# A convolution and mixture-of-experts block on one core: the experts in two passes, weights laid out on the host, and another order in the last iteration

## What is computed

```python
x = x + conv_ref(ln_c(x), ...)          # layer norm over channels, group norm, w1, relu, w2, residual
t = to_tokens(x)                        # 8 batches, 16384 tokens of 64 numbers
t = t + ffn_ref(ln_t(t), ...)           # layer norm over the 64 numbers of a token
# ffn_ref, per batch: 32 experts, each takes its K = 8 best tokens
logits = einsum('bsd,ed->bse', x, gate_w) + gate_b
vals, idx = top_k(softmax(logits, axis=1).transpose(0, 2, 1), 8)
pooled = einsum('bked,bke->bed', gathered, topv)
h = gelu(einsum('ebd,edh->ebh', [pooled, 1], weight1))   # weight1: 32 x 65 x 256
out = einsum('ebh,eho->ebo', [h, 1], weight2)            # weight2: 32 x 257 x 64
outputs = zeros.at[flat_idx].add(out * topv)             # 256 rows per batch
```

## Time and profile before

| | |
|---|---|
| median of 3 executions | 684.8 us (681.87 to 685.7) |
| the profiled execution: its own time, its span | 687.47 us, 685.7 us |
| busy share: PE, DVE, ACT, POOL | 79%, 71%, 62%, 27% |
| mean granted clock of the tensor engine | 0.893 |
| chain that ended last | PE 41%, DVE 36%, issue 8%, ACT 7% |

### The profile page before, as it was taken

How to read it: one execution, slowest core, us unless ns; L and a number is a source line. 1 busy time by engine, 2 the same in 40 slices (tenths; PEclk the granted TensorE clock), 3 DMA queues, 4 the chain that set the end, 5 groups by cost and what they waited for, 6 DMA issues and landing times.

```text
span 685.7 us, 13882 instructions
## 1 busy us (share of the span) xinstructions
PE 542.0 (79%) x5630; PEld 274.8 (40%) x5630; DVE 488.5 (71%) x946; ACT 426.1 (62%) x597; POOL 185.4 (27%) x110
## 2 busy tenths in 40 slices
PE   3569988988988898889888898989888476623981
PEld 1234444443444344444444443444334132321781
DVE  5674566898789688978897889688976276785120
ACT  1455787779767876797779777877796353431100
POOL 1008080216022502250244024302433500011044
PEclk9857999999999899999999999899999979955555
DMA  8940445344624462447145713471125941100000
GB/s 196 200 100 32 123 125 162 115 125 123 173 75 124 124 173 74 125 123 184 64 124 150 189 59 108 138 190 57 40 92 132 200 94 62 63 4 5 1 13 18
DMA packets 35428, 73.38 MB, mean 107 GB/s; under 512 B 12292, under 2 KB 14372, under 8 KB 31268
## 3 DMA queue, kind: packets, MB, share of 16 engines
q1 hardware_dynamic: 34340, 71.44, 38.8%
q0 software_dynamic: 1024, 1.05, 0.6%
HBM read 38.40 MB, written 34.08 MB: 106 GB/s over the span
## 4 chain that ended last, share of the span: by engine, by line
PE 41%; DVE 36%; issue 8%; ACT 7%; DMA 2%; another core or an unknown queue 2%; POOL 1%; SPq 0%; DVEq 0%; ACTq 0%; POOLq 0%
PE st L364 10%; DVE xs L856 7%; PE cv L375 6%; PE tl L392 6%; PE cv L383 6%; PE bc L483 5%; DVE us L846 5%; DVE us L848 4%; DVE top_i L943 4%; DVE lg L844 3%; ACT junk L722 3%; DVE cnd L938 3%; DMA xs<-in_x 1%; PE tl L401 1%
## 5 line engine op out<-in xcount | busy, mean ns | idle before, releaser
L1241 POOL TENSOR_TENSOR xs<-xs,us 128x1024 f32<-128x1024 f32 x64 | 150.6, 2378 | 375.3 <-DVE xs L856 179.2
L856 DVE SCALAR_TENSOR_TENSOR xs<-cv,vecs,xs 128x1024 f32<-128x1024 f32 x64 | 82.0, 1281 | 61.5 <-PE cv L383 47.5
L682 ACT ACTIVATE hid<-cv,b1n 128x1024 f32<-128x1024 f32 x64 | 71.3, 1113 | 47.4 <-PE cv L375 46.0
L715 ACT ACTIVATE sqc<-us 128x1024 f32<-128x1024 f32 x64 | 67.5, 1055 | 44.0 <-DVE us L846 43.2
L483 PE MATMUL bc<-rstd_s,spread 32*128 32x256 f32 x368 | 49.9, 350 | 55.6 <-DVE gsum L848 27.3
L848 DVE CUSTOM_DVE_ANT_0 us<-us,bc 128x1024 f32<-128x1024 f32 x60 | 72.9, 1215 | 22.3 <-PE bc L483 21.3
L392 PEld LDWEIGHTS tl<-ident,xs 128*128 128x128 f32 x512 | 65.0, 196 | 56.1 <-issue 56.0
L846 DVE TENSOR_TENSOR us<-xs,bc 128x1024 f32<-128x1024 f32 x60 | 72.9, 1216 | 19.3 <-PE bc L483 18.8
L722 ACT ACTIVATE junk<-us 128x1024 bf16<-128x1024 f32 x64 | 67.3, 1052 | 26.1 <-DVE gsum L848 25.3
L364 PE MATMUL st<-xs,stat_w 128*32 128x256 f32 x1024 | 75.1, 415 | 9.2 <-DMA xs<-in_x 9.0
L392 PE MATMUL tl<-ident,xs 128*128 128x128 f32 x512 | 77.9, 298 | 1.3 <-ACT lg L697 1.3
(11 more groups left out here) (186 smaller groups left out, 636.0 us busy)
## 6 DMA issues: line engine op xcount, KB each, us to landing
xs<-in_x SPq DMA_DIRECT2D x64, 512.0 KB, 7.0
out_rows<-tok SPq DMA_DIRECT2D x64, 512.0 KB
us<-in_e_w SPq DMA_DIRECT2D x4, 520.0 KB
xs<-in_e_w SPq DMA_DIRECT2D x8, 256.0 KB
sqc<-out_rows,idx_all POOLq DMA_INDIRECT x16
out_rows<-sqc,idx_all POOLq DMA_INDIRECT x16, 2.1
vecs<-in_b SPq DMA_DIRECT2D x4, 0.2 KB, 13.9
gate_bias<-in_gate_b SPq DMA_DIRECT2D x4, 0.1 KB, 12.3
```

The lines of the kernel that those rows point to most:

```text
L682: nc.scalar.activation(hid[:], cv[:], ACT.Relu, bias=b1n[:, par:par + 1]).then_inc(h_done, 1)
L856: nc.vector.scalar_tensor_tensor(out=xu, in0=cv[:], scalar=vecs[:, 3:4], in1=xu, op0=ALU.add, op1=ALU.add).then_inc(x1_done, 1)
L1241: nc.gpsimd.tensor_tensor(xu, xu, su, ALU.add).then_inc(s_done, 1)
```

## The change

Five things are changed. (1) The experts run in two passes, `PASSES`: batches 0 to 5 between the pieces of the search of batch 7, then 6 and 7. `add_rows` and `result_rows` take groups of batches, `ADDS`: 0 to 2, 3 to 5, 6, 7. (2) The weights come from the host in the layout of the on-chip memory (`e_w1` 65 x 32 x 256, `e_w2` 128 x 32 x 2 x 64, the bias row apart), in eight parts of two DMAs, one part in each step of the last iteration, behind the step's store; a contiguous run is 4 KB of `e_w1` and 2 KB of `e_w2`. (3) In the last iteration conv2 stands before `spread_pixels`, the diagonals are made in steps 1 to 3, the pairs are spread in steps 2, 4 and 5, and `ln2_rstd` stands behind `x1`. (4) In step 5 of every iteration from 1 on, `top_places` of the last piece stands behind `x1`. (5) A gather waits for the row numbers (`idx_out`) and no longer for the weights of the rows (`idx_ready`).

The core of the diff:

```diff
-ORDER = (0, 1, 5, 2, 3, 6, 4, 7)
+PASSES = ((0, 6), (6, 8))
+ADDS = ((0, 3), (3, 6), (6, 7), (7, 8))
-PAIR_AT, NORM_AT = (4, 5, 6), (4, 5, 6)
+DIAGS_AT, PAIR_AT, NORM_AT = (1, 2, 3), (2, 4, 5), (4, 5, 6)
...
 # sync engine: load_weights(part), now for 8 parts
-                e = slice(NE // 4 * part, NE // 4 * (part + 1))
+                e = slice(NE // 8 * part, NE // 8 * (part + 1))
-                sp.dma_start(ew1[:, e], e_w1[e].rearrange("e d n -> d e n")).then_inc(ew_in, 16)
-                for k in range(2):
-                    sp.dma_start(ew2[:, e, k, :], e_w2[e, k * P:(k + 1) * P, :].rearrange("e p o -> p e o")).then_inc(ew_in, 16)
+                sp.dma_start(ew1[:, e], e_w1[:, e]).then_inc(ew_in, 16)
+                sp.dma_start(ew2[:, e], e_w2[:, e]).then_inc(ew_in, 16)
...
-                if it == NB - 1 and 2 <= s <= 5:
-                    load_weights(s - 2)
                 if b >= 0:
                     store(b, u)
+                if it == NB - 1:
+                    load_weights(s)
...
 # tensor engine, step
+                if conv:
+                    conv2(it, s)
                 if not p1 and s in PAIR_AT:
                     spread_pixels(PAIR_AT.index(s))
-                if conv:
-                    conv2(it, s)
...
 # vector engine, step: top_places(t, 3) and ln2_rstd(7) move behind x1
-                if s == 5 and t >= 0:
-                    top_places(t, PLACES_AT[s])
-                if s == 6 and not p1:
-                    ln2_rstd(NB - 1)
                 use_at(it, (s, 0))
...
+                if s == 6 and not p1:
+                    ln2_rstd(NB - 1)
-                if t >= 0 and s in PLACES_AT and s != 5:
+                if t >= 0 and s in PLACES_AT:
                     top_places(t, PLACES_AT[s])
...
 # tensor engine, the tail
             tokens(NB - 1, 1, NU - 1)
             x1_sums(NB - 1, 1, NG - 1)
+            experts_in(0)          # pool_rows of batches 0 to 5
...
             logits(NB - 1, 1, NU - 1)
+            experts_up(0)
             for k in (2, 3):
                 spread_stat(NB, "E", k)
+            experts_turn(0)
+            experts_down(0)        # waits for all four turned blocks
+            expert_rows(0)
             spread_stat(NB, "M", NB - 1)
+            add_rows(0)
             spread_pixels(3)
+            experts_in(1)
+            experts_up(1)
+            experts_turn(1)
+            experts_down(1)
+            expert_rows(1)
+            add_rows(1)
...
 # scalar engine, the tail
+            for i in (0, 1):
+                explog(7, i)
+            gelu(0)                # loads the gelu table first
+            nc.scalar.preload_act_table_set("natural_log_exp_and_others")
+            for i in (2, 3):
+                explog(7, i)
             merge_exps(7)
             token_rsqrt(1, 6, NB)
+            gelu(1)
...
 # vector engine, the tail
+            pooled(0)
             top_values(7, 0)
             top_places(7, 0)
             ln2_variance(NB)
             top_values(7, 1)
+            ln2_rstd(NB)
             top_places(7, 1)
             use_spread(NB, "E", 2)
             merge_values(NB - 2, merging.pop(NB - 2))
             use_spread(NB, "E", 3)
+            top_values(7, 2)
+            top_places(7, 2)
+            turned(0)
+            top_values(7, 3)
+            top_places(7, 3)
+            expert_outs(0)         # 8 additions, before 2
+            candidates(7)
+            contributions(0)       # 1 product, before one per batch
             use_spread(NB, "M", NB - 1)
+            link = merge_pixels(NB, NB - 1)
+            merge_values(NB - 1, link)
+            diagonals(3)
+            for i in (0, 1):
+                result_rows(i)
+            equal_pixels(3)
+            token_norm(1, 6, NB)
+            pooled(1)
+            turned(1)
+            expert_outs(1)
+            contributions(1)
+            for i in (2, 3):
+                result_rows(i)
```

More of the change, by code:

```diff
@@ L588, in _, with experts_in, experts_up @@
                     step(it, s)
+            def experts_in(p):
+                pe.wait_ge(z_ready, p + 1)
+                if p == 0:
+                    pe.wait_ge(x1_done, NU * NB)
+                pool_rows(*PASSES[p])
+            def experts_up(p):
+                pe.wait_ge(pooled_ready, p + 1)
+                if p == 0:
+                    pe.wait_ge(ebias_ready, 1)
+                    pe.wait_ge(tok_done, NU * NB)
+                else:
+                    pe.wait_ge(row_ready, 2)
+                for e in range(NE):
+                    grp, slot = e // 4, e % 4
+                    mm = pe.matmul(h_banks[grp // 2][32 * slot:32 * slot + 32, HID * (grp % 2):HID * (grp % 2) + HID],
+                                   pool_f[:, NB * e:NB * e + 32], ew1[:, e, :], start=True, stop=True, skip_group_check=True)
+                    if e % 8 == 7:
+                        mm.then_inc(l1_done, 1)
@@ new lines, in expert_rows, with add_rows @@
+            def expert_rows(p):
+                b0, b1 = PASSES[p]
+                pe.wait_ge(eo_ready, p + 1)
+                for b in range(b0, b1):
+                    mm = pe.matmul(pt[:, C * (b - b0):C * (b - b0) + C], eot[:, P * b:P * b + P], id2[:], start=True, stop=True)
+                mm.then_inc(ob_done, 1)
+            def add_rows(p):
+                pe.wait_ge(z_done, p + 1)
+                pe.wait_ge(eq_ready, 3 + p)
+                for i in (2 * p, 2 * p + 1):
+                    for b in range(*ADDS[i]):
+                        for g in range(GATHERS):
+                            col = GATHERS * C * (b - ADDS[i][0]) + C * g
+                            for f in range(GATHERS):
+                                mm = pe.matmul(add_banks[i % 2][:, col:col + C], eq[:, b, f, P * g:P * g + P], zc[:, b, f, :],
+                                               start=(f == 0), stop=(f == GATHERS - 1))
+                    mm.then_inc(add_done, 1)
@@ L589, in _ @@
             tokens(NB - 1, 1, NU - 1)
             x1_sums(NB - 1, 1, NG - 1)
+            experts_in(0)
+            pe.wait_ge(ew_in, 16 * 17)
+            for h in range(HALVES):
+                mm = pe.matmul(pd[C * h:C * h + C, 0:NE], eb2, ident[0:NE, 0:NE], start=True, stop=True)
+            mm.then_inc(pex_done, 1)
             x1_square_sums(NB - 1, NG - 1)
             logits(NB - 1, 1, NU - 1)
+            experts_up(0)
             for k in (2, 3):
                 spread_stat(NB, "E", k)
-            pe.wait_ge(ew_in, 16 * 13)
@@ L1148, in _ @@
             use_spread(NB, "E", 3)
-            for i in (2, 3):
-                top_values(7, i)
-                top_places(7, i)
-            lns(nc.vector.tensor_tensor(id2[:], ident[:, 0:C], ident[:, C:P], ALU.add))
-            candidates(7)
-            use_spread(NB, "M", NB - 1)
-            merge_values(NB - 1, merge_pixels(NB, NB - 1))
-            diagonals(3)
-            dve.wait_ge(pex_done, 1)
-            nc.vector.tensor_copy(eb2t, pt[:, 0:NE]).then_inc(ebias_ready, 1)
-            token_norm(1, 6, NB)
@@ L1195, in _ @@
-            contributions(0)
-            for i in range(NB):
+            lns(nc.vector.tensor_tensor(id2[:], ident[:, 0:C], ident[:, C:P], ALU.add))
+            top_values(7, 2)
[6 more added lines that the diff above has]
+            contributions(0)
+            use_spread(NB, "M", NB - 1)
+            link = merge_pixels(NB, NB - 1)
+            merge_values(NB - 1, link)
@@ L1273 @@
     from concourse.bass_utils import run_bass_kernel_spmd
+    w2 = np.asarray(L0_ffn_weight2)
     ins = {
```

181 lines of the change are left out of this document (76 added, 105 removed).

## The result

The changed kernel takes **660.15 us** (median of 4 runs, 659.54 to 660.94), the kernel before 683.34 (4 runs, 680.77 to 685.7): ratio 0.966, 95% interval 0.962 to 0.970. Ratios leave out executions more than 1.5% above the fastest of their kernel, which are one in run 3 and one in run 7. The forecast was 658.5, the range 649 to 673. The profiled execution took 660.21 us with a span of 658.5, 27.2 less than the 685.7 before.

What follows compares the result with a forecast made beforehand. No engine is full, so the prediction asked which waits of the last 170 us end last. Steps 2 to 7 give 18.4 us and the tail 7.9, together 26.3: 684.8 - 26.3 = 658.5 us, range 649 to 673.

Steps and rivals of the forecast that it cites:

- The stall: Before `x1` of step 3, last iteration: 12.12 us idle behind 256-byte packets, taken as gone; steps 2 to 7 gain 18.4.
- rival (a): The stall stays, from the 12 gathers or a full DMA: 13.7 us of gain lost, 672 us; chance 0.14.
- Steps 4 to 7: Last iteration, each step's own work: 7.75, 9.9 and 8.0 us, the last two gaining nothing from reordering.
- `top_places`: Moved behind `x1` of step 5 in the six earlier iterations: 0 us, bounds 0 to 5 us slower.
- The tail: Everything behind `x1` of step 7 in the last iteration: 89.3 us for 97.2, so 7.9 us less.
- The new wait: In the tail, the vector engine waits 4.3 us for pass 0's down matmuls, ahead of the small additions.
- the down pass: In the tail, the 128 down matmuls of each pass take 7.0 us, paid again in full for two batches.
- rival (b): Tail costs more or less: no gain there, 666 us, chance 0.08; tensor engine at 2.4 GHz, 647, chance 0.05.
- the gather's wait: Gathers waiting on row numbers only save the four short instructions of `merge_values`, 0.8 us.
- The table load: Scalar engine, before pass 0's gelus: 1.28 us without drain; by the skill's page gelus come 1.4 us later.
- Rival (c): Eight weight parts stall the last iteration's instruction queue instead of three: slower, 690 us; chance 0.04.
- Rival (d): Pass 0's down matmuls or pooling wait for the last weights, passes don't overlap: with rival (a) about 684; chance 0.03.

Runs made afterwards that it cites:

- run 3: The changed kernel with its 12 gathers in three groups of four, the later groups waiting for `x1` of steps 3 and 4: 652.59 us, ratio 0.950.
- run 7: The kernel before with the down matmuls waiting at their start for all four turned blocks: 686.60 us, ratio 0.9999.
- 1: The kernel before with only `top_places` of the last piece moved behind `x1` in step 5: 676.62 us, ratio 0.986.
- 2: The kernel before with only the weights laid out on the host and loaded in eight parts behind the stores: 686.85 us, ratio 1.0008.
- 5: The kernel before with the whole change except the two passes and the gather's wait: 669.05 us, ratio 0.973.
- 11: The changed kernel measured again, unchanged: 660.62 us, ratio 0.963.
- 10: The changed kernel with its 12 gathers in two rows of six, the second waiting for `x1` of step 3: 653.52 us (one run).
- 6: The kernel before with its gathers in three groups of four, 256-byte weight rows kept: 679.04 us, ratio 0.988.
- 8: The changed kernel with gathers placed singly behind GpSimd's additions, `token_rsqrt(0)` later and `token_norm(1)` earlier: 648.87 us, ratio 0.947.
- 4: The changed kernel without gathers and scatters for batches 0 to 5, so its outputs are incomplete: 646.93 us (one run).
- 9: The changed kernel with gathers among GpSimd's additions in groups of 4, 4 and 2, scatters from the seventh delayed, norm and square root moved: 646.38 us, ratio 0.944.

## Why the prediction was right in the time and wrong in its terms

*The stall.* The failed step is "I read the stall as engines that wait for their instructions behind thousands of 256-byte packets", and with it "I take the stall as gone". The runs show another cause: a long row of indirect DMAs on GpSimd. Rows of 12 cost 8.1 to 12.2 us of idle vector engine (the kernel before, 1, 2, 5, 7, 11 and the changed kernel), of six 1.9 and 3.3 (10), of four none, with small packets (6) or without (3). Step 2 to 3 took 16.57 us for a forecast of 6.4, and 3 to 4 took 9.78 for 7.3: behind the idle time the granted clock was 0.50, as rival (a) said. The stall so kept 10.2 + 2.5 = 12.7 us of the gain. The cause that rival (a) named, "it may come from the 12 gathers", is the one that held; its time of 672 did not, since only this term differed from the forecast there. My argument against it, that later gathers stop nobody, was read from later gathers that come in pairs, and a pair says nothing of a row of twelve.

*Steps 4 to 7.* Forecast 7.75, 9.9 and 8.0; measured 7.74, 10.69 and 7.99. The 0.8 us too little is in `token_rsqrt`, on which the relu of step 6 waits; 8 moves it away and brings that step to 7.24. Steps 2 to 7 without a stall take 40.8 us (4) against my 39.3, so had the cause been right, the gain would have been 16.9 of 18.4. With the stall's 12.7 us these 0.8 make the 13.5 us by which steps 2 to 7 are over.

*`top_places`.* The failed step is "`x1` of step 5 waits for conv2 there anyway, so nothing is won". I read that from iteration 6, where step 4 to 5 takes 9.05 us and `x1` does wait 0.30 us for conv2. Iterations 1 to 5 have no wait there. Taken at 0 with bounds on the slower side only, the term measured -9.8 us (1), outside its bounds. In the profiled executions it is the 8.9 us before step 2. That the sum came out right is luck: these 8.9 us and 5.4 more in the tail than the 7.9, neither of them forecast, stand against the 13.5 of steps 2 to 7.

*The tail.* 83.9 us for 89.3. The new wait is there: the vector engine stands 1.63 us for the down matmuls of pass 0, not 4.3, the eight small additions take 1.54 us (I took 1.5), and `token_norm(1)` starts at T0+46.7 (forecast 50.3), long after its rows. That its late start is what the tail pays for was forecast and is not borne out: in 8 it starts 5.6 us earlier and the tail is 0.9 us shorter, since the DMAs of GpSimd then hold up the experts. The term that was mis-sized is the down pass, 7.0 us by the earlier trace rows, where 4.18 and 4.27 were measured:

```profile
599.00:601.00 2.00, 2.00 (x76) 2.00 (x72) 1.16 (x2) 0.77 (x1) 0.00 (x0) 1.00 0.04 8
605.00:615.00 10.00, 9.96 (x44) 9.19 (x44) 6.02 (x22) 0.51 (x2) 2.88 (x3) 0.50 0.04 7
```

In the first stretch, in the midst of the down matmuls of pass 0, the granted clock is 1.00 (0.92 and 0.89 over the whole of the two passes, since it rises just after their start and falls just before their end). It is 0.50 in the sums between, and was 0.50 in the down matmuls before:

```profile
644.00:650.00 6.00, 6.00 (x117) 6.00 (x116) 0.08 (x1) 0.00 (x0) 0.00 (x0) 0.50 0.01 3
```

That is 2.8 and 2.7 us. `token_norm(1)` starts 3.6 us before its forecast, 2.8 of them from pass 0. From there to the end 1.8 us are saved: the 2.7 of pass 1, less 1.1 ahead of those matmuls, where the scalar engine is late (see below), and 0.2 more behind them. A faster down pass was named in rival (b). It is no gift of the passes: 1, 5 and 7 have it too with one pass (4.58, 4.17, 4.17), and 2 and 6 don't (7.00). What is the passes' own, with the gather's wait, is what 5 leaves out: its tail is 667.8 - 575.2 = 92.6 us with the faster down matmuls, and 83.9 after, 8.7 less.

*The table load.* I took 1.28 us with no drain. The rows above show the load at 591.59 and the gelu at 592.89, 0.02 us behind its end; its matmuls had ended at 587.3, so nothing else hid a drain. The 2.66 us of the Trainium skill (ScalarE: Activation LUTs, section What ACT_TABLE_LOAD costs) is not what this trace shows; the gelu would have started at 594.25 by it.

*The rest.* Rival (c), stalls that grow with the number of parts, falls with 2: eight parts, one stall, as long as before. Rival (d) did not occur: the last weights landed in time. Its time with (a) was also summed wrong: 684.8 - 18.4 + 13.7 is 680, not 684. The gather's wait, 0.8 us, was changed in no run by itself and stays an estimate; it is on no path here, since `token_norm(1)` starts long after the rows have landed.

*What stays open.* First, how a row of indirect DMAs stops the other engines. The profile calls the wait "remote" or "issue", and the vector, scalar and tensor engine all stand. How much a row costs varies, and it can hide from one engine's rows. In the tail of the changed kernel 14 indirect DMAs go out one behind the other:

```profile
611.50 0.94 POOL L1270 DMA_INDIRECT sqc<-out_rows,idx_all  x1 [26.75 <-DVE idx_all L999]
...
628.04 0.96 POOL L1303 DMA_INDIRECT out_rows<-sqc,idx_all  x1 [0.30 <-issue]
```

The vector engine loses little beside them: its waits called "issue" there end with results that it needs. But the scalar engine's first gelu of pass 1 starts 2.8 us after the matmuls that feed it have ended (626.73 + 1.94), 2.5 us behind the row:

```profile
626.73 1.94 PE L608 MATMUL st<-us,lg 65*32 65x256 f32 x16 [0.36 <-issue]
631.46 0.60 ACT L832 ACTIVATE us<-st 128x512 f32<-128x512 f32 x1 [6.14 <-PE tl L608]
```

In 4, without the 12 scatters, it starts 0.06 us after them:

```profile
616.37 1.94 PE L608 MATMUL st<-us,lg 65*32 65x256 f32 x16 [0.36 <-DVE lg L1171]
618.37 0.60 ACT L832 ACTIVATE us<-st 128x512 f32<-128x512 f32 x1 [3.42 <-PE st L608]
```

So this row costs the changed kernel some 1.2 us (13.7 us for 12.5 from the pooling to the down matmuls), and in 8, where it meets more of the work, several. That engines wait for instructions, which come in packets of some 16 KB (0.74 MB in 45) and would stand behind the indirect DMAs, would fit, but it was only argued; no run changed when an engine fetches. The packets of the instruction queue say little for it, 1 in 23 us where 1.5 would be the average. Second, why the same 128 down matmuls run at 2.4 GHz in one kernel and at 1.2 in the next, behind a tensor engine as busy (5.0 of the 9.6 us ahead of pass 0 in the changed kernel, 5.2 of 9.4 in 4): neither the number of passes nor the wait ahead of them decides it.

## What to carry to other kernels

Where several engines wait for "remote" or "issue" at once, look at what GpSimd issued in the 5 to 7 us before: here long rows of indirect DMAs held up the vector engine for 10 us and the others beside it for much of that time, and rows of four with a wait on a later step between them did not. Work that is moved earlier can land beside such a row and lose what it gained, as in the tail of 8. Before an order is costed at nothing because "it waits there anyway", read that wait in every iteration and not in the one nearest the change. And where a sum comes out right, check its terms all the same: here an error of +13.5 us stood against two of -8.9 and -5.4 us.

## What the runs showed of the hardware that was not expected

**Rows of indirect DMAs.** 12 gathers in 15.4 us (520.99 to 536.41) left the vector engine idle from 528.1 to 538.4, with the DMA engines at a share of 0.66 and 0.32, and the granted clock fell from 1.00 to 0.50. Two rows of six stopped it for 1.9 and 3.3 us, a row of eight in the tail of 9 made it 2.2 us late, rows of four stopped it not at all; the scalar engine waited for "remote" behind rows of four too, 0.6 to 0.8 us in 3 and 6 and 2.4 in 9. The waits of the vector engine before `x1` begin 5 to 7 us into a row and end 1.1 to 2.4 us behind it (before: the row ends at 544.76, `x1` starts at 547.01); in 5 `x1` started 0.3 us before the end of the row, and a second wait followed.

**GpSimd holds up small vector instructions.** In 8, a `tensor_scalar` on 128x32 that takes 0.17 us in 9 took 2.77, and a `scalar_tensor_tensor` on 128x1 took 2.70; they end 0.05 and 0.03 us after the GpSimd addition beside them (496.68 + 2.37 and 501.44 + 2.36). SBUF — State Buffer, section Who interferes with whom, of the Trainium skill describes such a lock between the two engines, held for a whole instruction; the trace agrees as to the common end. The starts it does not show so clearly: both vector instructions begin 0.35 and 0.31 us before the addition's row does, beside the end of a gather. The same section says that "PE and ACT never wait on anyone", which is meant of SBUF's ports: a reader should not take it to cover the 2.4 us of TensorE in 9 or the scalar engine in the stall.

**The clock in short dense stretches.** The 128 down matmuls took 7.00 us in the kernel before, in 2, 6, and in pass 0 of 4 and 9, and 4.17 to 5.0 elsewhere (pass 1 of 9, with its gaps, aside); the granted clock was 0.50 throughout in the one case and on the mean 0.74 to 0.92 in the other, with 1.00 in the midst of them. The difference of up to 2.8 us per pass is more than several of the terms that the prediction worked out to a tenth.
